# Expert attention on four 32-column tiles, the causal attention moved directly behind it, a value projection moved one slot earlier

## The reference, cut to what matters

```
def _L0_attn_ref(x, WQ, WK, WV, WO):            # 16 heads of 16 columns, causal
    Q, K, V = (heads(WQ), heads(WK), heads(WV))
    score = softmax(einsum('bhqd,bhkd->bhqk', Q, K) / sqrt(D_K) + mask)
    out = einsum('bhqk,bhkd->bhqd', score, V)
    return out @ WO

def _moe_attn(x, Wq, Wk, Wv, Wo, Wsel_v, Wsel_o):   # 16 heads of 64 columns, 8 experts, top 2
    q, k = _rope(x @ Wq), _rope(x @ Wk)
    v = einsum('bsd,bhse,hedp->bhsp', x, gv, Wv)    # gv: gates of the chosen experts
    att = softmax(einsum('bhsp,bhtp->bhst', q, k) / sqrt(P))
    o = einsum('bhst,bhtp->bhsp', att, v)
    return einsum('bhsp,bhse,hepd->bsd', o, go, Wo)

x = x + _L0_attn_ref(xn, ...) + _L0_ffn_ref(xn, ...)
```

## Time and profile before

| | |
|---|---|
| median of three runs | 3404.74 us (3403.65 to 3405.85) |
| span of the profiled execution, first to last instruction | 3401.4 us |
| PE busy with matmuls | 3233.1 us (95%) |
| DVE, ACT, POOL busy | 2439.7 us (72%), 1961.5 us (58%), 1441.9 us (42%) |
| AT (L773), busy | 233.8 us in 1024 records, 16 to an item |
| AC (L785), records of 512, 384, 256 and 128 columns | busy 67.3, 53.7, 38.5, 24.9 us, 256 records each |

### The profile page before, as it was taken

How to read it: one execution, slowest core, us unless ns; L and a number is a source line. 1 busy time by engine, 2 the same in 40 slices (tenths; PEclk the granted TensorE clock), 3 DMA queues, 4 the chain that set the end, 5 groups by cost and what they waited for, 6 DMA issues and landing times.

```text
span 3401.4 us, 64468 instructions
## 1 busy us (share of the span) xinstructions
PE 3233.1 (95%) x18240; PEld 2378.9 (70%) x18240; DVE 2439.7 (72%) x4708; ACT 1961.5 (58%) x4509; POOL 1441.9 (42%) x1215
## 2 busy tenths in 40 slices
PE   1699999999999999999999999999999999997998
PEld 1577777777777777777777777777777777775765
DVE  6577777777777777777777777777777777775554
ACT  2466666656666666666666666666666666664121
POOL 4144355445443454345543554434534543442212
PEclk9999999999999999999999999999999999999999
DMA  5223333334233333233233332333332433333221
GB/s 165 76 71 87 95 90 85 77 76 109 76 84 87 84 98 81 75 100 96 69 87 76 96 98 77 76 104 81 84 87 68 114 81 75 84 75 110 72 83 62
DMA packets 115937, 295.18 MB, mean 87 GB/s; under 512 B 33856, under 2 KB 54592, under 8 KB 99264
## 3 DMA queue, kind: packets, MB, share of 16 engines
q1 hardware_dynamic: 115904, 294.78, 32.9%
HBM read 262.74 MB, written 31.98 MB: 87 GB/s over the span
## 4 chain that ended last, share of the span: by engine, by line
PE 85%; issue 6%; DVE 5%; ACT 3%; DMA 1%; POOL 0%; ACTq 0%; SPq 0%; DVEq 0%; POOLq 0%
PE bank L673 27%; PE bank L799 22%; PE bank L718 9%; PE bank L773 7%; PE bank L688 5%; PE bank L905 4%; PE bank L897 3%; PE bank L693 3%; PE bank L745 2%; PE bank L754 2%; ACT probs L957 2%; DVE uf L1239 1%; DVE oo L1232 1%; PE bank L694 1%; ACT pt_e L977 1%
## 5 line engine op out<-in xcount | busy, mean ns | idle before, releaser
L573 POOL TENSOR_TENSOR u_l<-uf,u_h 128x512 fp32r<-128x512 f32 x512 | 716.1, 1409 | 722.6 <-ACT u_h L1041 722.4
L1136 DVE TENSOR_REDUCE nmax<-bank 128x1 f32<-128x512 f32 (+3 forms) x1024 | 551.8, 579 | 305.0 <-PE bank L688 297.8
L673 PE MATMUL bank<-wv_h,xx 128*128 128x512 f32 x2048 | 755.0, 410 | 7.1 <-DVE vm L1157 7.1
L957 ACT ACTIVATE probs<-bank,nmax 128x512 f32<-128x512 f32 (+3 forms) x1024 | 590.7, 610 | 253.2 <-DVE nmax L1136 253.1
L1041 ACT ACTIVATE u_h<-uf 128x512 fp32r<-128x512 f32 x512 | 321.7, 632 | 696.9 <-DVE uf L1239 683.6
L673 PEld LDWEIGHTS bank<-wv_h,xx 128*128 128x128 f32 x2048 | 386.0, 188 | 155.8 <-issue 59.6
L718 PEld LDWEIGHTS bank<-ident_sb,probs 128*128 128x128 f32 x3328 | 388.3, 141 | 106.4 <-issue 51.3
L718 PE MATMUL bank<-ident_sb,probs 128*128 128x128 f32 x3328 | 451.3, 274 | 1.6 <-ACT stackT L1032 0.9
L569 POOL TENSOR_TENSOR v_sb<-v_next,zero_hb 128x512 f32<-128x512 f32 x64 | 74.2, 1160 | 891.9 <-PE bank L773 877.4
L799 PE MATMUL bank<-u_h,wo_h 128*128 128x512 f32 x1024 | 427.1, 417 | 5.0 <-ACT u_h L1041 3.2
L1239 DVE TENSOR_TENSOR uf<-oo,go 128x512 f32<-128x512 f32 x512 | 416.2, 823 | 8.8 <-POOL u_l L573 6.6
(11 more groups left out here) (141 smaller groups left out, 5164.2 us busy)
## 6 DMA issues: line engine op xcount, KB each, us to landing
go<-go_d SPq DMA_DIRECT2D x256, 512.0 KB, 6.5
xx<-xs_d SPq DMA_DIRECT2D x128, 512.0 KB, 3.5
oo<-scale_d SPq DMA_DIRECT2D x128, 128.0 KB, 2.9
a_d<-a_out SPq DMA_DIRECT2D x128, 128.0 KB, 2.3
pt_c<-in_x SPq DMA_DIRECT2D x16, 512.0 KB, 4.7
st<-in_wv SPq DMA_DIRECT2D x16, 512.0 KB, 5.8
st<-in_wo SPq DMA_DIRECT2D x16, 512.0 KB, 7.2
go_d<-go_turned SPq DMA_DIRECT2D x256, 8.0 KB
```

The lines of the kernel that those rows point to most:

```text
L573: nc.gpsimd.tensor_tensor(u_l[:, e % 2], uf[:, e % 2], u_h.bitcast(f32)[:, e % 2], ALU.subtract).then_inc(ul_done, 1)
L673: last = nc.tensor.matmul(out, lhs, rhs, start=n == 1, stop=n == 3 * len(chunks))
L957: nc.scalar.activation(probs[:, s % 2, j, 0:w], sbank[j][:, 0:w], ACT.Exp, bias=nmax[:, 2 * s + j:2 * s + j + 1], **kw).then_inc(exp_done, 1)
L1136: nc.vector.tensor_reduce(nmax[:, 2 * s + j:2 * s + j + 1], sbank[j][:, 0:w], AX.X, ALU.max, negate=True).then_inc(nmax_ready, 1)
```

## The change

The expert attention (AT) is issued as 16 matmuls on tiles of 32 columns where it was 8 on tiles of 64 columns; the rows that stream and the output are the same. In the list of PE's jobs AC moves from slot 1 to the end of slot 0, directly behind AT, and V1 moves from slot 2 to slot 1, behind V0. No other engine's list, no semaphore and no buffer changes.

```
-PE_FILL = [[("P", 0), ("P", 1), ("P", 2), ("P", 3), ("AT", 0)],
-           [("AC", 0), ("V", 0)],
-           [("J", 0), ("V", 1), ("J", 1)],
+PE_FILL = [[("P", 0), ("P", 1), ("P", 2), ("P", 3), ("AT", 0), ("AC", 0)],
+           [("V", 0), ("V", 1)],
+           [("J", 0), ("J", 1)],
...
                     for k in range(TT):
                         for j in range(2):
-                            mm = nc.tensor.matmul(o[j * P:(j + 1) * P, :], v_sb[:, k, j, :], pt_e[:, j, k, :], start=k == 0, stop=k == TT - 1)
+                            for c in range(0, P, STRIP):
+                                mm = nc.tensor.matmul(o[j * P + c:j * P + c + STRIP, :], v_sb[:, k, j, c:c + STRIP], pt_e[:, j, k, :], start=k == 0, stop=k == TT - 1)
                     mm.then_inc(w_full, 1)
```

## The result

The changed kernel takes 3443.38 us (median; 3442.72 to 3445.0), the kernel before, timed with it, 3404.93 us. The ratio is 1.0113 (95% interval 1.0099 to 1.0127), that is 38.5 us slower where 44 us were forecast.

A forecast was written before the change was run, and what follows sets the result against it. PE, busy 95% of the span, was taken as the bound. 62 inner items by 0.76 us gave +47 us, FIRST took 3 off: 3404.7 + 44 = 3449 us, range 3438 to 3462 us.

The forecast's parts named there:

- V1 waits for the copy of AC: Inner item, slot 1: PE reaches V1 at 1532.50 and waits 1.55 us for ACT's copy to a_out.
- The chain stays although the scores 2 come later: Inner item, DVE and ACT: scores 2 come 1.11 us later, yet the end of the chain from AT stays.
- 0.82 us late at the transposes of slot 2: Inner item on PE: these transposes start at 1539.03 against 1538.21 before, 0.82 us later.
- A little comes back: Inner item, J2 to the next transposes: J3's wait for u_l goes, some 0.05 us, leaving about 0.76 us.
- FIRST and the ends: First and last items: V1 fills 1.4 us of a PE wait in FIRST, LAST gains nothing; 3 us taken off.
- AT on four tiles costs nothing: AT in each item: four tiles stream as fast as two, no change, plus or minus 2 us in all.
- AC's saving never reaches the end: AC behind AT: 1.11 us against 1.21, but PE only waits 0.1 us longer at V1.
- The rival "not slower": V1 in inner items: its bank is free in time, about 0.1 us an item left to gain, 3396 us; chance 0.04.
- The rival of the clock: PE in inner items: 1.55 us of idling brings half clock, 1.7 us an item, 3554 us; chance 0.03.

The follow-up runs named there:

- e1: Kernel before with only the new order of PE's jobs (AC behind AT, V1 behind V0), AT still on 64-column tiles: 3442.9 us, ratio 1.0116.
- e2: Kernel before with only AT on 32-column tiles, the order of PE's jobs as before: 3402.43 us, ratio 0.9997.
- e4: Changed kernel with ACT's copy of AC to a_out moved later, behind the short copies VA and PA: 3479.24 us, ratio 1.0215.
- e3: Changed kernel with ACT's copy of AC to a_out moved sooner, ahead of the two u_h copies: 3405.69 us, ratio 1.0004.
- e5: Kernel before with u_l of experts 3 and 4 each moved ahead of rotary products on POOL: 3393.82 us, ratio 0.9963.
- e9: e5 plus, on DVE, the gate product of expert 3 moved ahead of V0's gate: 3393.49 us, ratio 0.9964.
- e8: e6 plus, on DVE, the gate product of expert 3 moved ahead of V0's gate: 3333.77 us, ratio 0.9794.
- e10: e8 with AT back on 64-column tiles, as in the kernel before: 3348.03 us, ratio 0.9825.
- e6: Changed kernel with AC's copy ahead of the u_h copies on ACT, and e5's order of POOL's list: 3373.85 us, ratio 0.9903.

## Why the prediction was right

The time, the sign and the mechanism were right; two terms were mis-sized, one of them in its sign as well. Their errors partly cancel: the inner items cost 37.8 us where the sum had 47, the rest of the program added 1.8 us where the sum took 3 off. So the total is closer than the terms, and that much of it is luck.

- *V1 waits for the copy of AC.* Shown: the wait goes with the order (e1, e2), grows with the copy (e4), goes with it (e3).
- *The chain stays although the scores 2 come later.* Right: the copy ended 1534.00 - 1528.05 = 5.95 us behind the end of AT in the forecast and 5.99 in the trace.
- *0.82 us late at the transposes of slot 2.* Measured 0.81.
- *"A little comes back", 0.05 us at J3.* Too low: 0.18 us came back. The step set two J of the LAST item, which follow the scores and so start after a break, against J2 and J3, which follow V2 without one, so that the 2.91 us held a cost of their own; without J3's wait J2 and J3 take 2.81 us (e5), and the wait cost 0.15 us. This term is most of the miss in the steady part, 62 by 0.13 = 8 us.
- *"FIRST and the ends", -3 us.* Wrong in sign: the first AT is 1.8 us later. Of this 0.7 us are there already in the prologue: the row at 128.90 stands at 129.63 in the changed kernel. That is scatter and not the change, for in e2, e5 and e9, which have the old order, it stands at 130.20, 130.02 and 129.53. The other 1.1 us arise in FIRST. V1 does fill the wait of the scores 3, from 3.25 us to 1.92, but slot 2 has no job left in FIRST, so the scores 4 now wait as well, and the lower clock, which lasted 3.4 us before, lasts 6.8 us. How the 1.1 us divide between this wait and the clock is not shown. PE and the window of the changed kernel:

```profile
129.63 0.22 PE L693 MATMUL bank<-stackT 96*128 96x128 bf16 x1 [2.35 <-ACT probs L958]
...
141.10 0.28 PE L693 MATMUL bank<-stackT 96*128 96x256 bf16 x1 [1.92 <-ACT probs L958]
...
145.47 0.80 PE L688 MATMUL bank<-k_h,q_h 64*128 64x512 f32 x2 [1.90 <-ACT probs L958]
```

```profile
142.00:148.80 6.80, 4.91 (x18) 3.47 (x17) 5.66 (x12) 2.94 (x8) 0.30 (x1) 0.50 0.00 0
```

- *AT on four tiles costs nothing.* Right: 595 ns a record by the groups view, 598 before. The loss that the Trainium skill measured for three column tiles ("TensorE: Matmul & The Clock Gate", Measured speedup vs the span model) does not show here.
- *AC's saving never reaches the end.* Right for the changed kernel: e1 has the turn of shapes and the same time. Where PE has no wait (e8 and e10) the turn from AT's shape to AC's is worth 0.16 us an item by the rows. The Trainium skill says in "TensorEngine Tiling (Array Packing)", Key Properties, that a change of tiling mode drains the engine; these rows agree with it.
- *The rival "not slower".* e3 is that case: V1's wait is gone, and J3's `u_l` takes all of the gain over the kernel before. It gave 3406 us where 3396 were worked out: J3 starts 15.03 us behind the end of AT in e3 and 15.00 before, so the 0.1 us an item that the rival still counted did not come, nor did the 3 us of FIRST.
- *The rival of the clock.* Not at 1.5 us of waiting; in e4 behind five of its waits of about 1.96 us.

So the changed order is not slow by itself. It needs the copy of AC sooner on ACT, `u_l` of expert 3 sooner on POOL and its gate product sooner on DVE; with all three it is e8, at 3333.77 us faster than both kernels. Without the changed order the same lists end at 3393 us.

## What to carry to other kernels

When a job is moved on the busiest engine, look up what must have left its bank by then and where that copy stands in the other engine's list; a wait that disappears may be only the first of two, as the wait of the scores 3 was here. Put each due time on one clock from a common event: here everything up to J3 counts from the end of AT, so without V1's wait (e3) the kernel was only back at its old time, and the further gains came from what J3 waits for (e6, e8). In these traces a wait of TensorE costs more than the idling shown, and a short one does not show at all.

## What the runs showed of the hardware that I had not expected

- A wait of PE in a stream of 512-column matmuls cost the idling shown and about 0.25 us more (e6 to e8: 0.39 us shown, 0.65 us gained).
- In e4 PE waits for `a_out` 56 times between 300 and 3000 us, 109.5 us in all, 1.96 us each. Five of these waits (one is the 1.87 us shown) were followed by 3.4 us at a granted clock of 0.50, the others were not. The waits of 1.5 us in the changed kernel never were, nor one of 2.35 us in the prologue. What sets the five apart, no run shows.
